# Weaving the preparations of a group's two tiles in stage 2 of a macaron layer on one core

## The chip, the cores and the metric

The kernel runs on 1 core of one Trainium2 chip. The metric is the device time of the whole program in microseconds (us), the median of several runs. TensorE (PE) multiplies matrices, with a separate row for its weight loads (PEld); VectorE (DVE), ScalarE (ACT) and GpSimd (POOL) work elementwise; SyncE (SP) issues all of this kernel's DMAs, in one queue, in program order. Each engine runs its own instructions in order, and semaphores tie them together.

## The reference, cut to what matters

The input is x of 2 batches, 2048 tokens and width 1024. A feed-forward block stands before and after an attention block:

```python
x = x + 0.5 * ffn(layernorm(x))
x = x + attn(layernorm(x))
x = x + 0.5 * ffn(layernorm(x))

def ffn(x):                                   # the token-wise part
    thought = agg of the LAST token; 4 steps of layer_norm -> d1 (1024x4096) -> gelu -> d2
    gate = sigmoid(x @ gate_w + gate_b)
    return layer_norm(x + gate * broadcast(thought @ bc_w + bc_b)) * out_gamma + out_beta

def attn(x):                                  # blocks of 128 tokens: own block and the one before
    q, k, v = split(x @ w_attn.T)
    sim = masked(q @ k2.T / 128);  a = relu(sim) ** 2
    return (a @ v2) @ w_o.T
```

## The kernel before

All tokens are cut into 32 tiles of 128 tokens, and tiles go in pairs: 16 groups of GROUP = 2 tiles, two batches in turn, from the last tokens to the first. Stage 1 (to about 713 us of the profiled execution) folds the attention's weights (wq with wk, wv with wo) and computes the first block's gates. Stage 2 (713 to 1655 us) takes the 16 groups through attention. Stage 3 (to the end) computes the second block's gates and the output. The "thought", the chain that only the last token of each batch needs, is a long series of small matmuls whose weights stream in from memory (`thought_units`); its second round is woven through stage 2 (pieces whose names begin with t_).

The order of all work is one list, PLAN, made by functions of Python. Every engine walks this list and emits its own part of each piece, so a place in the list is a place in each engine's queue. `plan_stage_2` takes for each group n the products of group n (`plan_products`, `plan_attention`) and weaves into them the preparation of group n + 1 (`plan_prep`) with `paced(..., 1.3, PE_PIECES)`: after each PE piece the next 1.3 pieces of the preparation follow. A piece ("rest",) emits nothing; it only takes a place. The last gates of stage 1 carry the preparation of group 0 in the same way.

A group from n = 3 on has 30 PE pieces: 8 q (24 matmuls 128x256 each), 9 v (three values of the four, each in thirds of 8 matmuls 128x512), 6 score, 3 v, 4 collect. Their results go to four PSUM banks in turn (`product_banks`). Banks are emptied by ACT (high part, 16 bit) and then DVE (low part): q_low is L1747, v_low L1788, score L1762, L1765 and L1777, collect L1797. In each group q takes banks 0 to 3, the three values 0 to 2, the first score 3, the second score 0, the last value 1. The score also waits for all four q_low.

A tile u of a preparation passes through:

- prep_fetch (L1020, L1024): SP fetches x (px) and the stage-1 gate (pg) of both tiles of the next group; this stands at the end of a group. The pg slot is free when the group before has been transposed.
- prep_norm (ACT L1430), prep_h (DVE L1701, needs pg), prep_beta (DVE L1708), prep_y (DVE L1714, then moments L1547 and following).
- prep_x1 (DVE L1723, L1728), prep_stats (DVE L1547 and following, then POOL), x1_store (SP L1043).
- prep_h1 (ACT L1438, L1441, needs POOL's statistics), prep_low (DVE L1738).
- group_turn (SP L1037): a transposing DMA into `gate_arena` (the first two groups: `thought_units`). The first q of a group waits for both tiles' transposes.

The thought's pieces in this stretch: t_low (DVE L1953; then SP stores the result, L993, and fetches on, L899), t_pair and t_unit (PE L1315), t_mean and t_var (PE L1285, and short DVE work).

Of the kernel before, what the change touches and what calls it, by code (L numbers as in the profile page):

```python
# [21 lines left out]
GROUP = 2  # L22
# [382 lines left out]

def plan_prep(n):

    out = []
    for i in range(GROUP):
        u = n * GROUP + i  # L410
        out += [("prep_norm", u), ("prep_h", u), ("rest",), ("prep_beta", u), ("prep_y", u), ("rest",), ("prep_x1", u),
                ("prep_stats", u), ("rest",), ("x1_store", u), ("prep_h1", u), ("rest",), ("prep_low", u),
                ("group_turn", u)]
    return out


def plan_value(n, i, h):
# [70 lines left out]
def plan_stage_2(first, last):  # L488
    out = []
    for n in range(first, last):  # L490
        out += [("prep_fetch", n + 1)]
        products, values = plan_products(n)
        out += paced(products + plan_attention(n, values), plan_prep(n + 1), 1.3, PE_PIECES)
    return out
# [61 lines left out]
def whole_plan():  # L556
# [37 lines left out]
    before = [(kind, u) for kind in ("prep_norm", "prep_beta") for u in range(GROUP)]  # L594
    prep = [("rest",)] + [("prep_norm", 1), ("prep_beta", 1)] + [("rest",)] * 3
    prep += [p for p in plan_prep(0) if p not in before]
    late = []
    for n in range(LATE):
# [1488 lines left out]
```

## Time and profile before

| | us |
|---|---|
| median of 3 runs | 1989.63 (1988.72 to 1992.05) |
| the profiled execution, its own time | 1999.55 |
| its span | 1998.3 |
| PE busy in the span | 1944.7 (97%) |
| DVE busy | 1300.3 (65%) |
| ACT busy | 662.8 (33%) |
| POOL busy | 166.4 (8%) |

The time of a run and the span of its profile differ by 1.25 us of work around the program. The profiled execution is 9.9 us longer than the median, so differences are worked out in the profiled execution and then taken off the median. A row of a timeline gives the start, the time from the first instruction's start to the last one's end, the line, the operation, the tiles and, in brackets, idle time of that engine just before and who ended it. L numbers are lines of the kernel before; in the changed kernel everything below `plan_prep` stands one line higher.

### The profile page before, as it was taken

Reading aid. Unit: us, or ns where it says so; the run is one execution under the profiler, and the core shown is the slowest. Engines: PE = TensorE matmul, PEld = TensorE weight load, DVE = VectorE, ACT = ScalarE, POOL = GpSimd, SP = SyncE. Lnnn points to the kernel's source line nnn. Section 1 sums busy time; section 2 is a strip of 40 time slices with the busy share of each in tenths; the row PEclk is TensorE's granted clock in tenths of the full one; section 3 lists DMA queues with packets and bytes.
Section 4 is the critical chain, followed back from the end, with each engine's and each line's share of the span. In section 5 each row is a group of like instructions: output and inputs, shape, how many; then the busy total and the mean of one; then the engine's idle time right before and its main releaser. Section 6 shows DMA issues by size and latency. Waiting matters only on the chain.

```text
span 1998.3 us, 30999 instructions
## 1 busy us (share of the span) xinstructions
PE 1944.7 (97%) x12136; PEld 1034.7 (52%) x12136; DVE 1300.3 (65%) x2318; ACT 662.8 (33%) x961; POOL 166.4 (8%) x278
## 2 busy tenths in 40 slices
PE   8999999999999999999999999999999999999997
PEld 3334444444444466666556566556655564444443
DVE  2656687224444666777877756757657638888887
ACT  1455456213333322224343221222112213444442
POOL 0000001000000100110100000100000001111111
PEclk9999999999999999999999999999999999999999
DMA  9899987889899753389979899998999965555552
GB/s 362 315 343 351 384 307 292 309 313 359 349 407 392 295 190 106 97 286 342 304 260 341 272 373 315 322 312 306 319 333 300 337 227 171 149 155 151 158 148 74
DMA packets 275217, 555.81 MB, mean 278 GB/s; under 512 B 149040, under 2 KB 149248, under 8 KB 274688
## 3 DMA queue, kind: packets, MB, share of 16 engines
q1 hardware_dynamic: 275072, 553.83, 79.4%
q8 instruction: 97, 1.59, 0.3%
q14 instruction: 48, 0.39, 0.1%
HBM read 406.93 MB, written 113.26 MB: 260 GB/s over the span
## 4 chain that ended last, share of the span: by engine, by line
PE 36%; DMA 7%; DVE 6%; SPq 2%; ACT 1%; issue 1%; POOL 0%; DVEq 0%; ACTq 0%
PE product_banks L1116 32%; DMA thought_units<-parts_scratch 3%; PE thought_acc L1315 2%; PE product_banks L1250 2%; DMA arena<-gate_scratch 1%; DVE bn_parts L1547 1%; DMA thought_units<-in_d_w 1%; DMA arena<-in_x 1%; DVE thought_units L1953 1%; SPq L1037 1%; SPq L899 1%; DMA gate_arena<-arena 1%; DVE arena L1728 1%; DVE arena L1723 1%; DVE arena L1714 0%
## 5 line engine op out<-in xcount | busy, mean ns | idle before, releaser
L1116 PE MATMUL product_banks<-gate_arena,arena 128*128 128x512 f16 x1536 | 347.8, 381 | 0.0
L1116 PE MATMUL product_banks<-wide_a,thought_units 128*128 128x512 f16 x1536 | 331.7, 379 | 0.0
L1116 PE MATMUL product_banks<-gate_arena,wide_a 128*128 128x256 f16 x2688 | 303.4, 274 | 8.2 <-DMA gate_arena<-arena 8.2
L1116 PE MATMUL product_banks<-wide_b,gate_arena 128*128 128x512 f16 x1344 | 299.2, 379 | 0.0
L1116 PEld LDWEIGHTS product_banks<-gate_arena,wide_a 128*128 128x128 f16 x2688 | 261.6, 98 | 54.2 <-issue 22.3
L1116 PEld LDWEIGHTS product_banks<-gate_arena,arena 128*128 128x128 f16 x1536 | 148.4, 99 | 191.8 <-issue 31.0
L1116 PEld LDWEIGHTS product_banks<-wide_a,thought_units 128*128 128x128 f16 x1536 | 150.3, 98 | 181.2
L1116 PEld LDWEIGHTS product_banks<-wide_b,gate_arena 128*128 128x128 f16 x1344 | 129.5, 98 | 157.4 <-issue 11.3
L1547 DVE BATCH_NORM_STATS2 bn_parts<-arena 128x6 f32<-128x512 f32 x256 | 164.2, 683 | 4.6
L2017 POOL TENSOR_TENSOR token_stats<-stats,minus_half 128x1 f32<-128x1 f32 x96 | 65.2, 679 | 991.8 <-DVE stats L1555 814.0
L1572 DVE SCALAR_TENSOR_TENSOR arena<-product_banks,inverse_gate,arena 128x512 f32<-128x512 f32 x64 | 48.0, 749 | 131.5 <-PE product_banks L1116 104.0
L1147 PE MATMUL product_banks<-wide_a,wide_b 128*128 128x512 f32 x256 | 120.7, 619 | 5.8 <-DMA wide_a<-in_w_attn 5.8
L2017 POOL TENSOR_TENSOR stats<-stats,minus_half 128x1 f32<-128x1 f32 x64 | 65.7, 1027 | 671.4 <-DVE stats L1555 387.0
L1453 ACT ACTIVATE gate_arena<-product_banks 128x256 f16<-128x256 f32 x128 | 41.3, 379 | 203.7 <-PE product_banks L1116 203.7
L1315 PE MATMUL thought_acc<-thought_units,thought_parts 128*6 128x512 f16 x1356 | 96.1, 379 | 6.4 <-DMA thought_units<-parts_scratch 5.0
L1459 ACT ACTIVATE arena<-product_banks 128x512 f16<-128x512 f32 x64 | 38.1, 597 | 182.8 <-PE product_banks L1116 182.8
L1493 ACT ACTIVATE arena<-arena 128x512 f32<-128x512 f32 x64 | 40.4, 632 | 168.3 <-DVE arena L1572 168.3
L1430 ACT ACTIVATE arena<-arena,token_stats 128x1024 f32<-128x1024 f32 x32 | 39.6, 1236 | 168.1 <-DMA arena<-in_x 168.1
L1701 DVE TENSOR_TENSOR arena<-arena,thought_row 128x1024 f32<-128x1024 f32 x32 | 39.0, 1219 | 84.9 <-DMA arena<-gate_scratch 84.9
L1250 PE MATMUL product_banks<-arena,key_weights 128*128 128x512 f16 x372 | 86.0, 384 | 4.7 <-DVE key_weights L1777 3.3
L1147 PEld LDWEIGHTS product_banks<-wide_a,wide_b 128*128 128x128 f32 x256 | 47.9, 196 | 67.9 <-issue 67.9
L1116 PE MATMUL product_banks<-gate_arena 128*128 128x256 f16 x672 | 78.1, 273 | 0.0
(223 smaller groups left out, 2357.5 us busy)
## 6 DMA issues: line engine op xcount, KB each, us to landing
thought_units<-parts_scratch SPq DMA_DIRECT2D x275, 512.0 KB, 7.6
thought_units<-in_d_w SPq DMA_DIRECT2D x174, 512.0 KB, 7.0
arena<-in_x SPq DMA_DIRECT2D x64, 512.0 KB, 9.3
parts_scratch<-thought_units SPq DMA_DIRECT2D x64, 512.0 KB, 6.1
x_scratch<-arena SPq DMA_DIRECT2D x64, 512.0 KB, 8.2
thought_row<-in_d_w SPq DMA_DIRECT2D x50, 512.0 KB, 7.0
arena<-x_scratch SPq DMA_DIRECT2D x40, 512.0 KB, 7.5
gate_scratch<-arena SPq DMA_DIRECT2D x32, 512.0 KB, 8.3
```

What stands on the lines that cost most here:

```text
L1116: mm = pe.matmul(bank, left(i, k), right(j, k), start=(n == 0), stop=(n == 3 * KD - 1))
L1147: mm = pe.matmul(bank_ap(key), wide_b[:, e, d * P:(d + 1) * P], wide_a[:, e, h * BANK:(h + 1) * BANK], start=(e == 0), stop=(e == KD - 1))
L1250: mm = pe.matmul(bank_ap(key), weights_of(u, side)[:, i], value_parts(other)[:, j, h * BANK:(h + 1) * BANK], start=(side == n == 0), stop= ...
L1315: mm = pe.matmul(thought_acc[at:at + PARTS * B, :], value, unit[:, part, h * BANK:(h + 1) * BANK], start=first and part == 0, stop=last an ...
L1430: act.activation(ph_slots[u % PREP_RING], px_slots[u % PREP_RING], ACT.Identity, bias=st[:, 1:2], scale=st[:, 0:1]).then_inc(h0_made, 1)
L1453: act.activation(queries[:, query_place(n * GROUP + i), 0, e - 1:e + 1, :], made[:, i], ACT.Copy, scale=QUERY_SCALE).then_inc(q_high_made, 1)
L1459: act.activation(value_parts(n * GROUP + i)[:, 0, h * BANK:(h + 1) * BANK], bank_ap(key), ACT.Copy, scale=VALUE_SCALE).then_inc(value_high, 1)
L1493: act.activation(res, res, ACT.Sigmoid).then_inc(gated_3, 1)
L1547: dve.bn_stats(bn_parts[:, h, :], source[:, h * BANK:(h + 1) * BANK]).then_inc(own.up(), 1)
L1572: dve.scalar_tensor_tensor(out=res[:, cols], in0=bank_ap(key), scalar=inverse["gate"][:, :], in1=bias[:, cols], op0=ALU.mult, op1=ALU.add) ...
L1701: dve.tensor_tensor(gb, gb, thought_row[:, GROUP_OF[u // GROUP][0], :], ALU.mult).then_inc(gate_spread, 1)
L2017: return pool.tensor_tensor(to, st[:, 2:3], minus_half[:, 0:1], ALU.pow)
```

## The change

`plan_prep` is rewritten. Before, tile u and tile u + 1 each had a run of 14 places, one after the other, with four rests each: 28 places. Now the list is written out once for the two tiles u and w, with 24 places, four of them rests: the pieces of w start inside those of u. The pieces, their instructions and their buffers are the same; only their places in the list move. At 1.3 places a PE piece, the last one, group_turn of w, comes after 18.5 PE pieces instead of 21.5.

```diff
 def plan_prep(n):
 
-    out = []
-    for i in range(GROUP):
-        u = n * GROUP + i
-        out += [("prep_norm", u), ("prep_h", u), ("rest",), ("prep_beta", u), ("prep_y", u), ("rest",), ("prep_x1", u),
-                ("prep_stats", u), ("rest",), ("x1_store", u), ("prep_h1", u), ("rest",), ("prep_low", u),
-                ("group_turn", u)]
-    return out
+
+    u, w = n * GROUP, n * GROUP + 1
+    return [("prep_norm", u), ("prep_h", u), ("rest",), ("prep_beta", u), ("prep_y", u), ("prep_norm", w), ("prep_h", w),
+            ("prep_x1", u), ("prep_stats", u), ("prep_beta", w), ("prep_y", w), ("x1_store", u), ("prep_h1", u),
+            ("prep_x1", w), ("prep_stats", w), ("prep_low", u), ("group_turn", u), ("rest",), ("x1_store", w),
+            ("prep_h1", w), ("rest",), ("rest",), ("prep_low", w), ("group_turn", w)]
```

DVE, near the end of the preparation of tiles 10 and 11 inside group 4 (931 to 990 us). Before; L1788 is a v_low of group 4, L1953 a t_low, L1762 and L1765 the first score of group 4, L1738 the prep_low of tile 11:

```order
841 L1788 SCALAR_TENSOR_TENSOR arena<-product_banks,arena 128x512
842 L1953 SCALAR_TENSOR_TENSOR thought_units<-thought_units,unit_scale 128x1024
843 L1762 SCALAR_TENSOR_TENSOR key_weights<-product_banks,score_scale,keep_own 128x128
844 L1765 SCALAR_TENSOR_TENSOR product_banks<-key_weights 128x128
845 L1762 SCALAR_TENSOR_TENSOR key_weights<-product_banks,score_scale,keep_prev 128x128
846 L1765 SCALAR_TENSOR_TENSOR product_banks<-key_weights 128x128
847 L1953 SCALAR_TENSOR_TENSOR thought_units<-thought_units,unit_scale 128x1024
848 L1738 SCALAR_TENSOR_TENSOR arena<-arena 128x1024
```

The same place in the changed kernel (lines one lower); the first L1737 is the prep_low of tile 10, the second that of tile 11, and the three v_low of group 4 stand between them:

```order
828 L1973 TENSOR_TENSOR hidden<-part_sums,d_bias 128x16 x2
829 L1546 BN_STATS bn_parts<-arena 128x6 x2
830 L1548 BN_AGGR stats<-bn_parts 128x2
831 L1551 TENSOR_SCALAR stats<-stats 128x1
832 L1556 TENSOR_SCALAR stats<-stats 128x1
833 L1737 SCALAR_TENSOR_TENSOR arena<-arena 128x1024
834 L1787 SCALAR_TENSOR_TENSOR arena<-product_banks,arena 128x512 x3
835 L1737 SCALAR_TENSOR_TENSOR arena<-arena 128x1024
836 L1952 SCALAR_TENSOR_TENSOR thought_units<-thought_units,unit_scale 128x1024
837 L1761 SCALAR_TENSOR_TENSOR key_weights<-product_banks,score_scale,keep_own 128x128
```

The prep_low of tile 11 moved ahead of two t_low and of the first score's four instructions; the three v_low moved behind all of both tiles' other preparation.

SP, the same stretch. Before; the first L1037 transposes tile 10 and the second tile 11, L1043 stores x1 of tile 11:

```order
432 L1037 DMA_TRANSPOSE gate_arena<-arena 128x16x128
433 L1058 DMA arena<-x_scratch 128x1024 x2
434 L899 DMA thought_units<-parts_scratch 128x1024 x2
435 L993 DMA parts_scratch<-thought_units 128x1024
436 L899 DMA thought_units<-in_d_w 128x1024
437 L1043 DMA x_scratch<-arena 128x1024
438 L993 DMA parts_scratch<-thought_units 128x1024
439 L899 DMA thought_units<-in_d_w 128x1024
440 L1037 DMA_TRANSPOSE gate_arena<-arena 128x16x128
```

The same place in the changed kernel:

```order
432 L1036 DMA_TRANSPOSE gate_arena<-arena 128x16x128
433 L1042 DMA x_scratch<-arena 128x1024
434 L1057 DMA arena<-x_scratch 128x1024 x2
435 L898 DMA thought_units<-parts_scratch 128x1024 x2
436 L992 DMA parts_scratch<-thought_units 128x1024
437 L898 DMA thought_units<-in_d_w 128x1024
438 L1036 DMA_TRANSPOSE gate_arena<-arena 128x16x128
439 L992 DMA parts_scratch<-thought_units 128x1024
440 L898 DMA thought_units<-in_d_w 128x1024
```

The transpose of tile 11 moved ahead of one store of the thought and its fetch, but one such pair still stands ahead of it; the store of x1 moved to just behind the transpose of tile 10. PE's own queue is the same instruction for instruction.

## Rows read from the trace of the kernel before

**Rows 1.** The page, busy time, share of the span and instructions.

```profile
PE 1944.7 (97%) x12136; PEld 1034.7 (52%) x12136; DVE 1300.3 (65%) x2318; ACT 662.8 (33%) x961; POOL 166.4 (8%) x278
```

**Rows 2.** Who PE waited for, 700 to 1660 us: total, times, longest.

```profile
PE product_banks L1116 <- DMA gate_arena<-arena: 8.2, 5, 2.7
PE thought_acc L1315 <- DMA thought_units<-parts_scratch: 5.0, 7, 2.0
PE product_banks L1250 <- DVE key_weights L1777: 3.3, 2, 2.2
PE thought_turn L1285 <- DVE thought L1993: 2.3, 3, 1.1
PE product_banks L1250 <- DVE arena L1788: 1.2, 1, 1.2
...
PE product_banks L1116 <- DVE gate_arena L1747: 0.6, 1, 0.6
```

**Rows 3.** Timeline of PE at three of these waits, start and length first.

```profile
762.28 2.29 PE L1250 MATMUL product_banks<-arena,key_weights 128*128 128x512 f16 x5 [2.21 <-DVE key_weights L1777]
...
990.54 0.80 PE L1116 MATMUL product_banks<-gate_arena,wide_a 128*128 128x256 f16 x4 [2.24 <-DMA gate_arena<-arena]
...
1472.95 1.25 PE L1116 MATMUL product_banks<-gate_arena,wide_a 128*128 128x256 f16 x10 [2.73 <-DMA gate_arena<-arena]
```

**Rows 4.** Stretches: length, busy time of the engines (instructions), granted clock, DMA share, GB/s.

```profile
762.00:766.00 4.00, 3.72 (x10) 1.40 (x11) 1.42 (x3) 0.53 (x1) 0.00 (x0) 0.57 1.06 314
...
990.50:994.00 3.50, 3.46 (x18) 2.55 (x19) 3.41 (x7) 0.00 (x0) 0.00 (x0) 0.54 0.90 294
```

**Rows 5.** Timeline of SP, issues of tiles 10 and 11, then of tile 27.

```profile
965.53 6.06 SPq L1037 DMA_TRANSPOSE gate_arena<-arena  x1
...
979.95 0.32 SPq L993 DMA_DIRECT2D parts_scratch<-thought_units  x1
...
981.37 6.96 SPq L1037 DMA_TRANSPOSE gate_arena<-arena  x1
...
1459.15 11.55 SPq L1037 DMA_TRANSPOSE gate_arena<-arena  x1
```

**Rows 6.** Timeline of DVE inside group 4, the preparation of tiles 10 and 11.

```profile
943.87 1.23 DVE L1701 TENSOR_TENSOR arena<-arena,thought_row 128x1024 f32<-128x1024 f32 x1 [7.91 <-DMA arena<-gate_scratch]
...
964.87 1.22 DVE L1701 TENSOR_TENSOR arena<-arena,thought_row 128x1024 f32<-128x1024 f32 x1
966.01 0.68 DVE L1788 SCALAR_TENSOR_TENSOR arena<-product_banks,arena 128x512 f16<-128x512 f32 x1
...
976.28 1.28 DVE L1953 SCALAR_TENSOR_TENSOR thought_units<-thought_units,unit_scale 128x1024 f16<-128x1024 f32 x1
977.47 0.35 DVE L1762 SCALAR_TENSOR_TENSOR key_weights<-product_banks,score_scale,keep_own 128x128 f32<-128x128 f32 x1
...
979.99 1.23 DVE L1738 SCALAR_TENSOR_TENSOR arena<-arena 128x1024 f16<-128x1024 f32 x1
```

**Rows 7.** Stretches from the first L1701 to the last L1738 of a preparation; columns as in rows 4.

```profile
943.87:981.22 37.35, 37.35 (x266) 23.18 (x264) 34.80 (x56) 16.32 (x24) 4.46 (x6) 1.00 0.91 308
1424.39:1459.13 34.74, 34.22 (x255) 22.04 (x253) 31.27 (x69) 10.21 (x18) 3.23 (x7) 1.00 0.71 258
```

**Rows 8.** Timeline of PE around the scores of group 4.

```profile
970.39 1.04 PE L1116 MATMUL product_banks<-gate_arena 128*128 128x256 f16 x8
...
972.32 4.54 PE L1116 MATMUL product_banks<-gate_arena 128*128 128x256 f16 x40
```

**Rows 9.** Timeline of DVE: end of group 1's preparation, start of group 13's.

```profile
758.35 1.23 DVE L1738 SCALAR_TENSOR_TENSOR arena<-arena 128x1024 f16<-128x1024 f32 x1 [2.08 <-ACT arena L1441]
...
1424.39 1.23 DVE L1701 TENSOR_TENSOR arena<-arena,thought_row 128x1024 f32<-128x1024 f32 x1 [11.17 <-DMA arena<-gate_scratch]
```

**Rows 10.** Stretches by DMA share; columns as in rows 4.

```profile
1150.00:1250.00 100.00, 98.37 (x800) 63.22 (x799) 60.50 (x129) 20.24 (x39) 6.73 (x17) 1.00 0.99 345
...
1550.00:1600.00 50.00, 49.34 (x358) 26.64 (x356) 31.93 (x67) 10.04 (x17) 3.46 (x9) 1.00 1.01 334
```

## The prediction, written before the changed kernel ran

> **What bounds the kernel now.** I read the page's busy shares first, then who PE waited for in stage 2, then the timelines of PE, DVE and SP at the largest of those waits, and last the busy time of DVE over one preparation. PE is busy 1944.7 us of the span, 97% [rows 1]. The change moves no PE instruction, so what it can give is only PE's idle time in stage 2, and what it can take is new idle time there. The list of waits is the whole prize: 20.6 us from 700 to 1660 us if its lines are added, of which the largest is 8.2 us in five waits for a transpose into `gate_arena` [rows 2]. Each of these five is the first q of a group waiting for the second tile of its own preparation; two of them are seen at 990.54 (2.24 us) and 1472.95 (2.73 us) [rows 3]. The next lines are the thought's weights (5.0 us in seven waits), the score's low parts L1777 (3.3 us in two), the thought's DVE step L1993 (2.3 us in three), one v_low L1788 (1.2 us) and one q_low L1747 (0.6 us) [rows 2].
>
> Behind the transposes stands DVE. From the first instruction of tile 10 to the last of tile 11 it is busy 34.80 of 37.35 us, for tiles 26 and 27 31.27 of 34.74 us [rows 7]. So the second tile is late for two reasons: its pieces stand late in the list, and DVE has little air. Both count below.
>
> A second price hangs on two of the waits. Right behind the wait that ended at 762.28 the granted clock is 0.57 over 4 us, and behind the one that ended at 990.54 it is 0.54 over 3.5 us [rows 3, 4]; elsewhere in stage 2 it is at full speed. That is the lower of the two levels (1.2 instead of 2.4 GHz) for most of these stretches; the work lost is 4.0 x 0.43 = 1.7 us and 3.5 x 0.46 = 1.6 us. The wait at 1472.95 was longer and no low stretch followed, so a wait of this size may or may not bring one.
>
> **The transposes (removed: 8.2 us).** How much earlier is the second tile? Take group 4. In the changed order two t_low and the first score's four instructions no longer stand ahead of tile 11's L1738. By starts in rows 6, a t_low takes 977.47 - 976.28 = 1.2 us, twice 2.4; the four of the score end where the second t_low started, 978.65, so 1.2 us. The same busy time less these: 34.8 - 3.6 = 31.2, so L1738 of tile 11 would end at 943.87 + 31.2 = 975.1 instead of 981.2, if DVE never waits. It cannot come before the three v_low, whose last product is complete when the first score starts at 970.39 [rows 8]; that bound is the earlier one, so DVE decides. On SP one store and one fetch of the thought still stand ahead of the transpose: the store waits for a t_low that ends 1.2 us behind L1738, and store and fetch take 1.4 us (979.95 to 981.37 [rows 5]). So the transpose issues at 975.1 + 1.2 + 1.4 = 977.7 instead of 981.37, 3.7 us earlier. PE waited 2.24 us. The wait goes, with 1.4 us to spare. For tile 27 no such store stands ahead: 31.27 us of DVE less 1.3 for the first score ends L1738 at 1454.4 instead of 1459.1, 4.7 us earlier against a wait of 2.73 us [rows 3, 7]. The other three waits are shorter, 8.2 - 2.24 - 2.73 = 3.2 us together. I take all 8.2 us. From the other side the bound is 0: SP's issue of one transpose takes 6.06 to 11.55 us [rows 5], and the two of a group now stand closer, so a second one could queue behind a slow first.
>
> **The clock (removed: 3.3 us).** If the waits before 762.28 and 990.54 go, both low stretches go, 1.7 + 1.6 = 3.3 us. Bounds: 0 if some other gap brings them back, 3.3.
>
> **The collects (removed: 4.5 us).** At 758.35 DVE stood idle 2.08 us for ACT's half of tile 3's preparation, with L1738 ahead of the score's low part in its queue [rows 9]; PE then waited 2.21 us [rows 3]. In the new order this L1738 stands a PE piece behind the start of the first score, its ACT part two pieces before that, so it neither waits nor stands in the way: 2.2 us. The second L1777 wait (3.3 - 2.2 = 1.1 us) and the v_low one (1.2 us) come at the end of groups whose L1738 ran up to the collects; they go for the same reason, 2.3 us. Bounds 0 and 4.5.
>
> **What stays.** The waits for the thought's weights (5.0 us), for L1993 (2.3 us) and the one for q_low (0.6 us) are not touched by design. The three rests fewer in each tile and the second tile's store of x1, moved to just behind the first transpose on SP, cost nothing by themselves: a rest emits nothing, and the first tile's transpose, now three PE pieces later, was issued at 965.53 for a q at 990.54 [rows 3, 5]: 25 us, of which three of a group's 30 pieces (some 6 us) are a quarter.
>
> **What is added (about 5 us).** DVE now does both tiles' work before the first v_low of a group. In group 4 what stands behind this v_low inside the old stretch is two more v_low (0.6 us each by start to start [rows 6]), L1738 of tile 11 (1.2), two t_low (2.4) and the first score (1.2): 6.0 us. So it ends at 943.87 + 34.8 - 6.0 = 972.7 instead of 966.7. The second score needs its bank. It starts after the 16 remaining matmuls of the first, 16 x 4.54/40 = 1.8 us behind 972.32, at 974.1 [rows 8]: a margin of 1.4 us, where there were 7.4. In the four groups with t_low on DVE I allow 0.75 us each, 3 us in all; in the later ones the two t_low pairs ahead of it are absent and the margin is some 4 us wider. The thought's short DVE steps (L1993 and others) meet a denser DVE in the first half of a group and a freer one in the second; I allow 1 us. The DMAs are busy 0.99 and 1.01 of two stretches of stage 2 [rows 10], and all transfers must now fit a shorter time: 1 us more for the thought's weights. Bounds of the whole term: -2 (the fetches of the next group stand behind the last transpose on SP, so they go out earlier and DVE's stall at L1701, 7.91 us and 11.17 us [rows 6, 9], shrinks) and 15.
>
> **The sum.** 8.2 + 3.3 + 4.5 = 16.0 us removed, 5 us added, net 11 us: the profiled execution would take 1988.5 us instead of 1999.55, and the median 1989.63 - 11.0 = 1978.6 us. Its own range runs from 16 + 2 = 18 us less (1972) to 5 us less (1985).
>
> **Rivals.** *The gain is given back to the DMAs.* If the stretch from 850 to 1600 us is held by the thought's transfers, only what lies before 850 us is gained, 2.2 + 1.7 = 3.9 us: 1985.7 us. For it: the shares of 0.99 and 1.01 [rows 10]. Against: PE waits for these weights only 5.0 us in all [rows 2], and the share from 943.87 to 981.22 is 0.91 [rows 7]. A page of the Trainium skill speaks for it: "DMA: Bandwidth & Descriptors", section "Issuing engines are not separate DMA queues", says that all DMAs run on the same 16 engines and interleave there. The trace agrees in so far as the same transpose takes SP 6.06 us in one group and 11.55 us in another.
>
> *The second tile is not earlier.* If the store and fetch ahead of it on SP and the slow first transpose eat the 3.7 to 4.7 us, the 8.2 us and the 1.6 us of clock stay: 16.0 - 9.8 - 5 = 1.2 us less, 1988.4 us. Against: the margins above are worked out with them.
>
> *Slower: the first v_low comes too late.* DVE runs in order, and in all 13 groups from n = 2 on the second tile's L1701, which waits for its own fetch, now stands ahead of q_low and v_low of the running group. If DVE is L us later than I reckon at the first v_low, the second score waits L - 1.4 us in each: with L = 3, 13 x 1.6 = 20.8 us, less 16 gained, 4.8 us more: 1994.4 us. It is even at L = 2.6. For it: DVE busy 34.80 of 37.35 us [rows 7] and stalls of 7.91 and 11.17 us at L1701 [rows 6, 9]. Against: both fetches of a group are issued together, so the second is there soon after the first, and the groups without t_low have a wider margin. The Trainium skill, "TensorE: Matmul & The Clock Gate", section "Architectural detail: the array is 16x 32x32, not 1x 128x128", states that ScalarE and VectorE queues are strict FIFO; this is the mechanism of that rival, and the trace agrees: the q_low of group 4 ran only after the 7.91 us stall.
>
> **How the numbers follow.** The forecast has 0.70, the DMAs 0.13, the second tile not earlier 0.09, slower 0.08. This kernel's measurement can tell about 0.2% from no change, 4 us; faster means below 1985.65. The forecast and a little of the DMA rival lie there: 0.71. Same: the rest of it and the second tile, 0.21. Slower: 0.08. The range leaves out the slower rival and the far ends: 1971.5 to 1989.
>
> **What would show it.** In the profile after, the waits of PE for `gate_arena<-arena` should be under 1 us in all, the granted clock should not fall around the starts of groups 1 and 5, PE's idle time from 713 to 1655 us should be near 13 us instead of 20.6, and the transposes of second tiles should land 3 to 5 us ahead of the first q. New waits of PE on L1787 (v_low) at the second score would show the added term; above 15 us in all they would make the prediction wrong. So would waits for the thought's weights above 10 us.

## The result, and the profile after

The changed kernel is slower. Its median is 2026.17 us (2021.73 to 2028.32, four runs) against 1990.84 us (1988.72 to 1997.18, four runs) of the kernel before: ratio 1.0157, 95% interval 1.0138 to 1.0175. The ratio, which this text goes by, is some 31 us; the two medians stand 35.3 us apart. The forecast was 1978.6 us, the range ended at 1989.0.

The page of the changed kernel, the busy line (as [rows 1]) and the DMA's mean rate:

```profile
PE 1954.4 (96%) x12136; PEld 1038.1 (51%) x12136; DVE 1300.4 (64%) x2318; ACT 662.9 (33%) x961; POOL 193.1 (10%) x278
...
DMA packets 275217, 555.81 MB, mean 274 GB/s; under 512 B 149040, under 2 KB 149248, under 8 KB 274688
```

PE is busy 9.7 us longer with the same 12136 matmuls. DVE and ACT have not changed. The bytes are the same, and their rate fell only because the run is longer. The next two fences give all of stage 2 as one stretch, of after and then of before (columns as in [rows 4]).

```profile
700.00:1683.00 983.00, 942.72 (x6974) 592.13 (x6973) 644.33 (x1282) 243.94 (x399) 99.83 (x159) 0.98 0.81 273
```

```profile
700.00:1655.00 955.00, 933.55 (x6982) 589.64 (x6981) 646.67 (x1283) 244.00 (x400) 74.35 (x158) 1.00 0.84 281
```

The stretch grew by 28 us, as much as the whole span (2026.6 instead of 1998.3). So the loss is in stage 2, and it has two parts: PE stands idle 40.3 instead of 21.4 us (+18.9), and it works 9.2 us longer because its granted clock was lower. It stood on its low level for 37.5 us of this stretch, in seven pieces; before it was 6.8 us in two.

Who PE waited for after the change, 650 to 1700 us (total, times, longest; as [rows 2], lines one lower):

```profile
PE thought_acc L1314 <- DMA thought_units<-parts_scratch: 23.8, 10, 5.5
PE thought_turn L1284 <- DVE thought L1992: 4.7, 1, 4.7
PE product_banks L1115 <- DVE arena L1787: 4.5, 2, 2.6
PE product_banks L1249 <- DVE key_weights L1776: 1.4, 1, 1.4
PE product_banks L1115 <- DVE gate_arena L1746: 1.4, 1, 1.4
PE product_banks L1249 <- DVE arena L1787: 1.3, 1, 1.3
PE thought_acc L1304 <- DMA thought_units<-in_agg_w: 0.9, 1, 0.9
PE thought_turn L1284 <- DVE squares L1875: 0.8, 1, 0.8
PE product_banks L1115 <- DMA gate_arena<-arena: 0.8, 1, 0.8
```

The waits for the transposes, which the change was expected to remove, fell from 8.2 to 0.8 us. In their place stand 23.8 us for the thought's weights (5.0 before) and one wait of 4.7 us in the thought's DVE chain. By the starts of the groups' first q, groups 3 to 8 take 379.9 us instead of 357.5, and groups 9 to 15 with the end of the stage 430.0 instead of 424.8.

Two of the three largest new waits lie at the ends of groups 3 and 4 (the third, 4.67 us in the thought's DVE chain, comes further below). Timeline of PE after the change:

```profile
930.94 1.88 PE L1314 MATMUL thought_acc<-thought_units,thought_parts 128*6 128x512 f16 x16 [5.53 <-DMA thought_units<-parts_scratch]
...
994.25 1.88 PE L1314 MATMUL thought_acc<-thought_units,thought_parts 128*6 128x512 f16 x16 [3.87 <-DMA thought_units<-parts_scratch]
```

and timeline of SP ahead of the second of them, where [rows 5] has the same place of before:

```profile
975.53 0.43 SPq L992 DMA_DIRECT2D parts_scratch<-thought_units  x1
976.01 0.49 SPq L898 DMA_DIRECT2D thought_units<-in_d_w  x1
981.78 1.58 SPq L1036 DMA_TRANSPOSE gate_arena<-arena  x1
983.40 1.29 SPq L1042 DMA_DIRECT2D x_scratch<-arena  x1
984.80 1.83 SPq L1057 DMA_DIRECT2D arena<-x_scratch  x2
986.73 0.86 SPq L898 DMA_DIRECT2D thought_units<-parts_scratch  x2
```

From 976.50 to 981.78 SP issues nothing: it stands at the transpose of tile 10. What it waits for is on DVE, in the timeline of that engine:

```profile
952.71 1.22 DVE L1700 TENSOR_TENSOR arena<-arena,thought_row 128x1024 f32<-128x1024 f32 x1 [6.26 <-DMA arena<-gate_scratch]
...
980.54 1.22 DVE L1737 SCALAR_TENSOR_TENSOR arena<-arena 128x1024 f16<-128x1024 f32 x1
981.67 1.28 DVE L1787 SCALAR_TENSOR_TENSOR arena<-product_banks,arena 128x512 f16<-128x512 f32 x2
985.30 0.69 DVE L1787 SCALAR_TENSOR_TENSOR arena<-product_banks,arena 128x512 f16<-128x512 f32 x1 [2.35 <-ACT arena L1458]
985.90 1.22 DVE L1737 SCALAR_TENSOR_TENSOR arena<-arena 128x1024 f16<-128x1024 f32 x1
```

L1737 of tile 10 comes 27.8 us after the first L1700, since DVE has most of tile 11's preparation ahead of it by then. In the kernel before it came 17 us after it (960.81, with the first L1701 at 943.87). The transpose waits for it, and behind the transpose, in SP's queue, stands the fetch of the thought's weights that PE is going to need. The fetch goes out at 986.73, PE wants the weights at 990.38 and gets them at 994.25. Before, the same pair of fetches went out at 972.78. Group 4 itself begins 6.2 us later now (937.51, before 931.31), so counted from its first q the pair goes out after 49.2 us instead of 41.5:

```profile
971.70 0.99 SPq L1058 DMA_DIRECT2D arena<-x_scratch  x2
972.78 0.86 SPq L899 DMA_DIRECT2D thought_units<-parts_scratch  x2
```

The wait at the end of group 3 is read in the same way, and there the groups start almost together (873.73 and 873.15): the first transpose goes out at 914.13 instead of 903.33, the pair of fetches behind it at 922.74 instead of 914.29; the second of the pair lands at 930.80, and PE goes on at 930.94.

Over the stage SP stood for prep_low this long (waits of SP's queue, 700 to 1660 us), after the change and then before:

```profile
SPq L1036 <- DVE arena L1737: 121.4, 19, 16.6
```

```profile
SPq L1037 <- DVE arena L1738: 81.2, 19, 10.1
```

Counted as the gaps in SP's issues just before each transpose, it is 109 us after the change, 96 ahead of first tiles and 13 ahead of second ones, and 85 before, 46 and 39.

Each of the seven waits of 2.2 us or more in this stage ends in, or is followed by, a stretch at a low clock; none of the shorter ones has such a stretch to itself. At the two above, after the change (columns as in [rows 4]; the first stretch lies for the most part inside the wait itself, so PE is busy little in it):

```profile
928.00:932.00 4.00, 1.06 (x12) 0.42 (x16) 0.00 (x0) 0.00 (x0) 0.00 (x0) 0.50 1.12 277
930.90:935.50 4.60, 4.56 (x25) 1.54 (x26) 0.38 (x1) 0.00 (x0) 0.00 (x0) 0.60 1.14 286
994.20:998.50 4.30, 4.25 (x22) 1.30 (x23) 0.00 (x0) 1.15 (x1) 0.00 (x0) 0.50 1.13 358
```

The thought's 16 matmuls take 1.88 us there and 1.04 us at full clock elsewhere. Such stretches, 30.7 us more of them than before, are where PE's 9.7 us come from.

### The profile page after: what moved, and what is told of

Read it like the earlier page. It is cut to its first block, busy times and chain, and to the rows that moved or that the text cites. A ratio compares the mean times of both kernels' runs of the same rounds, so it can differ in the third digit from the quotient of the medians.

```text
span 2026.6 us, 30999 instructions
## 1 busy us (share of the span) xinstructions
PE 1954.4 (96%) x12136; PEld 1038.1 (51%) x12136; DVE 1300.4 (64%) x2318; ACT 662.9 (33%) x961; POOL 193.1 (10%) x278
## 2 busy tenths in 40 slices
DMA packets 275217, 555.81 MB, mean 274 GB/s; under 512 B 149040, under 2 KB 149248, under 8 KB 274688
## 4 chain that ended last, share of the span: by engine, by line
PE 37%; DVE 6%; DMA 5%; SPq 3%; issue 1%; ACT 1%; POOL 0%; ACTq 0%; DVEq 0%
PE product_banks L1115 33%; PE thought_acc L1314 2%; PE product_banks L1249 2%; DMA thought_units<-parts_scratch 2%; SPq L1036 2%; DMA arena<-gate_scratch 2%; DMA thought_units<-in_d_w 1%; DVE bn_parts L1546 1%; DVE thought_units L1952 1%; SPq L898 1%; DMA arena<-in_x 1%; DVE arena L1727 1%; DVE arena L1722 0%; DVE arena L1707 0%; DVE arena L1713 0%
## 5 line engine op out<-in xcount | busy, mean ns | idle before, releaser
L1115 PEld LDWEIGHTS product_banks<-wide_b,gate_arena 128*128 128x128 f16 x1344 | 130.3, 99 | 160.0 <-issue 15.7
L2016 POOL TENSOR_TENSOR token_stats<-stats,minus_half 128x1 f32<-128x1 f32 x96 | 81.7, 851 | 1127.3 <-DVE stats L1554 916.1
L1314 PE MATMUL thought_acc<-thought_units,thought_parts 128*6 128x512 f16 x1356 | 99.0, 389 | 25.1 <-DMA thought_units<-parts_scratch 23.8
L1787 DVE SCALAR_TENSOR_TENSOR arena<-product_banks,arena 128x512 f16<-128x512 f32 x64 | 43.3, 687 | 91.3 <-ACT arena L1458 91.3
L1700 DVE TENSOR_TENSOR arena<-arena,thought_row 128x1024 f32<-128x1024 f32 x32 | 39.0, 1218 | 85.1 <-DMA arena<-gate_scratch 85.1
```

The costliest lines, as they stand in the source:

```text
L1115: mm = pe.matmul(bank, left(i, k), right(j, k), start=(n == 0), stop=(n == 3 * KD - 1))
L1314: mm = pe.matmul(thought_acc[at:at + PARTS * B, :], value, unit[:, part, h * BANK:(h + 1) * BANK], start=first and part == 0, stop=last an ...
L1787: dve.scalar_tensor_tensor(out=parts[:, 1], in0=bank_ap(key), scalar=VALUE_SCALE, in1=parts[:, 0], op0=ALU.mult, op1=ALU.subtract).then_in ...
L2016: return pool.tensor_tensor(to, st[:, 2:3], minus_half[:, 0:1], ALU.pow)
```

## The experiments

Two theories stood against each other. **SP's queue**: the first tile's transpose waits longer for its prep_low, and the thought's fetches stand behind it. **DVE**: with four rests fewer and both tiles' work first, DVE is too dense or late for what PE and the thought need from it. In the expectations A and S are the first; B is the second; C says that SP's order is harmless and that only DVE's late prep_low costs, by making SP stand; D says that it is the second transpose, early on SP in front of a fetch that PE needs; E is a loss that stays in its group, F one that drags on, G one that is the same in every group. "Idle" below is PE's idle time from 700 us to the start of stage 3, "low" the time at the low clock there; before has 21.4 and 6.8 us, after 40.3 and 37.5. Ratios are against the kernel before on the same chip, with the 95% interval. u is a group's first tile, w its second.

**Fewer rests, old order.** Still tile after tile, two rests of four taken out of each.

```diff
-        out += [("prep_norm", u), ("prep_h", u), ("rest",), ("prep_beta", u), ("prep_y", u), ("rest",), ("prep_x1", u),
-                ("prep_stats", u), ("rest",), ("x1_store", u), ("prep_h1", u), ("rest",), ("prep_low", u),
+        out += [("prep_norm", u), ("prep_h", u), ("rest",), ("prep_beta", u), ("prep_y", u), ("prep_x1", u),
+                ("prep_stats", u), ("x1_store", u), ("prep_h1", u), ("rest",), ("prep_low", u),
```

> The old order, tile after tile, but with four rests instead of eight (24 places), so the second tile's transpose stands 12 PE pieces ahead of the next group as in the changed kernel, and the first tile's 21 ahead (20 before, 17 in the changed kernel). Theory A (what costs 35 us is the first tile's transpose, which is late and stands on SP in front of fetches that PE needs 11 us later): no cost here, and the 8.2 us of waits for transposes go: 1975 to 1990 us. Theory B (it is the shorter, denser preparation on DVE, whatever the order of the tiles): slower than before, 2005 us or more.

Measured: 2017.0 against 1995.46 us, 1.0109 (1.0084 to 1.0134); idle 32.9, low 27.3. The denser list alone, without weaving, costs 21.5 us (B's side). Its waits are of another kind: 7.9 us for L1993, 6.9 for v_low, 7.6 for the thought's weights, and none at the end of group 3. So the plan before is finely set, and moving the preparation in it in either manner has a price.

**Woven, but the first tile as early as before.** 24 places as in the change, with prep_low and group_turn of u back at their old distance from the end, those of w as in the change.

```diff
...
+            ("prep_x1", u), ("prep_stats", u), ("prep_h", w), ("x1_store", u), ("prep_h1", u), ("prep_beta", w),
+            ("prep_low", u), ("group_turn", u), ("prep_y", w), ("rest",), ("prep_x1", w), ("prep_stats", w),
+            ("x1_store", w), ("prep_h1", w), ("rest",), ("rest",), ("prep_low", w), ("group_turn", w)]
```

> Woven, 24 places, but the first tile's prep_low and transpose stand where they stood before (21 and 20 PE pieces ahead), the second tile's where the changed kernel has them (13 and 12). Theory A: PE's waits for the thought's parts fall from 23.8 us to under 8 and the time to 1980 to 1995 us. Theory B (dense DVE through weaving): stays above 2010 us, with waits on DVE or for the parts above 15 us.

Measured: 2003.69 against 1995.46 us, 1.0043 (1.0023 to 1.0063); idle 30.4, low 17.1. Of 31 us, 22 are gone, with the same number of rests, and the waits for the thought's weights fell from 23.8 to 10.3 us; both numbers lie between what A and B had forecast. The wait at the end of group 3 is gone. In group 4 SP now issues the transpose of u at 971.42 and the thought's fetches at 979.35:

```profile
971.42 5.88 SPq L1035 DMA_TRANSPOSE gate_arena<-arena  x1
977.35 0.58 SPq L1041 DMA_DIRECT2D x_scratch<-arena  x1
978.04 1.22 SPq L1056 DMA_DIRECT2D arena<-x_scratch  x2
979.35 1.58 SPq L897 DMA_DIRECT2D thought_units<-parts_scratch  x2
```

PE still waits 3.08 us for these weights, at 987.89. The run is the strongest evidence that the late first tile costs most of it. But this edit moves the tile on DVE and on SP together, and puts pieces of w behind it that stood ahead of it in the change.

**SP's order alone.** Five kernels let SP walk a list of its own, made with another plan_prep, while all other engines keep theirs:

```diff
+SP_PLAN = whole_plan()
...
-        for kind, *a in PLAN:
+        for kind, *a in SP_PLAN:
             if kind == "start":
```

The kernel before, SP in the changed order:

> All engines as in the kernel before, SP alone walks the order of the changed kernel. Theory A in its narrow form (the places on SP alone do it; the first transpose is ready but issued late, in front of the fetches): the waits for the thought's parts rise to 12 us or more, 2005 to 2020 us. Theory C (the order of SP is harmless, what costs is that DVE makes the first tile's prep_low 10 us later, so that SP stands at its transpose): within 8 us of before, 1983 to 1999 us.

Measured: 2012.86 us, 1.0090 (1.0074 to 1.0106); idle 29.8, low 27.3; 14.8 us for the thought's weights. No instruction of DVE, ACT or PE moved, and 17.4 us are lost, as A had it. In group 4 the thought's fetches go out at 977.19, 49.7 us after the group's first q (927.47), as late as in the changed kernel, and PE waits 6.86 us for them. But this isn't a share of the change's 31 us: there is no wait at the end of group 3, and SP stands 29 us ahead of first transposes and 54 us ahead of second ones, the other way round than in the changed kernel (96 and 13), since here the second one is asked for before DVE has made its tile.

The changed kernel, SP in the old order:

> All engines as in the changed kernel, SP alone walks the order of the kernel before: the first tile's transpose stands three PE pieces earlier on SP than DVE's prep_low for it. Theory A in its narrow form: back to 1985 to 2000 us. Theory C: SP now stands at the first transpose from an even earlier place until DVE has made prep_low, with still more fetches behind it: 2026 us or more.

Measured: 2036.05 us, 1.0208 (1.0187 to 1.0230); idle 46.2, low 37.5. SP stands 148 us ahead of first transposes, which are now asked for at the old early place while DVE makes them late, as C had it (whose range the kernel above had missed, 1983 to 1999 us). The order must fit the time at which tiles are ready, on both queues.

The woven list with the early first tile, SP in the old order:

> The engines as in e2 (woven, 24 places, first tile's prep_low where it was before, second tile's three PE pieces earlier), SP alone in the order of the kernel before: the second transpose stands 9 pieces ahead of the next group, behind the thought's fetch that the collects need, and finds its tile ready. Theory D (each place of a transpose on SP ahead of that fetch costs, because the next fetches stand behind its issue of 6 to 12 us): the cost of e2 goes, 1980 to 1996 us. Theory B (the denser DVE costs by itself): 2000 us or more, with waits on DVE as in e2 and few for the parts.

Measured: 2004.79 against 1993.57 us, 1.0057 (1.0039 to 1.0075); idle 26.5, low 10.2. The same as with SP in its own woven order (1.0043) within the intervals, where D had forecast that the cost would go. The waits for weights are down to 4.3 us; those for transposes are back, 10.0 us.

The kernel before, only the transpose of w four places earlier on SP (ahead of w's own store of x1 and of the thought's stores that stood before it), and, apart from it, only that of u four places later on SP, both from group 1 on:

> The kernel before; on SP alone the second tile's transpose moves from 9 to 12 PE pieces ahead of the next group (its prep_low is at 10 on DVE), past the thought's fetch. Theory D: the waits for the parts rise to 12 us or more and most of the 17 us of e3 is here, 2005 to 2015 us. Theory A (it is the first tile's transpose): within 5 us of before.

> The kernel before; on SP alone the first tile's transpose moves from 20 to 17 PE pieces ahead of the next group, with its tile ready since long. Theory A: 2003 us or more and waits for the parts above 12 us. Theory D: little, since no fetch that PE needs soon is passed: within 5 us of before.

Measured: w earlier 2007.47 us, 1.0065 (1.0046 to 1.0084), idle 28.8, low 17.1; u later 1998.49 us, 1.0023 (1.0010 to 1.0036), idle 22.9, low 13.7. By medians 13.9 and 4.9 us, about the 17.4 us of both together, as D had it. So of SP's order alone it is the second transpose that costs most. The first is plain to read. The transpose of w is asked for before w is ready, and SP stands (waits of SP's queue in that kernel, where before had 81.2 us; L1052 is its transpose):

```profile
SPq L1052 <- DVE arena L1753: 139.6, 24, 13.8
```

PE's list of waits in the same kernel:

```profile
PE thought_acc L1330 <- DMA thought_units<-parts_scratch: 12.1, 11, 2.4
PE thought_turn L1300 <- DVE thought L2008: 6.3, 3, 4.6
PE thought_turn L1338 <- DVE t_wide L1975: 3.3, 1, 3.3
```

No wait for a transpose is left, and it is slower by 14 us: 8.2 us of waits for transposes were exchanged for more waits for the thought.

**The changed kernel, the first transpose held behind the next fetch of the thought on SP.** From group 3 on.

```diff
+        if piece[0] == "group_turn" and piece[1] % GROUP == 0 and piece[1] >= 3 * GROUP:
+            held.append(piece)
+            continue
...
-        for kind, *a in PLAN:
+        for kind, *a in SP_PLAN:
```

> The changed kernel; on SP alone the first tile's transpose is held back, from group 3 on, behind the next fetches of the thought's products (at the latest to just before the second's). If the fetches behind the first transpose are what costs in the changed kernel (theory A), PE's waits for the parts fall from 23.8 us to under 12 and the time from about 2030 to 2005 us or less. If the cost is the late DVE or the second transpose, the time stays above 2018 us.

Measured: 2024.02 us, 1.0153 (1.0123 to 1.0183); idle 38.0, low 27.3. A cure by SP's queue alone failed (A had forecast 2005 us or less). It did what it should in the place at which it was aimed: SP stands 62.9 instead of 121.4 us for prep_low, and the wait at the end of group 3 is 1.22 instead of 5.53 us.

```profile
921.00 1.04 PE L1332 MATMUL thought_acc<-thought_units,thought_parts 128*6 128x512 f16 x16 [1.22 <-DMA thought_units<-parts_scratch]
```

```profile
912.87 10.02 SPq L1054 DMA_TRANSPOSE gate_arena<-arena  x2
922.94 0.81 SPq L1010 DMA_DIRECT2D parts_scratch<-thought_units  x1
```

But the two transposes then stand back to back and hold the queue for 10.02 us, and what comes behind them is late instead. The wait at the end of group 4 is gone. Waits for the weights went from 23.8 to 15.7 us, while waits for v_low rose from 5.8 to 8.3 us and those of L1340 for t_wide from 0.3 to 3.8 us. The time stayed.

**Where in the stage.** The woven list in some groups only, the old one in the others.

```diff
+def plan_prep(n):
+
+    return plan_prep_woven(n) if 3 <= n <= 8 else plan_prep_old(n)
```

Groups 0 to 2:

> The changed order for the preparations of groups 0 to 2 alone, the old one for all others. In the changed kernel's profile group 3 begins only 0.5 us later than in the kernel before. Theory E (the loss is local, it adds up over the groups): 0 to 4 us slower than before. Theory F (a late start of one group drags through all that follow): 15 us or more.

Groups 3 to 8:

> The changed order for the preparations of groups 3 to 8 alone, where the thought's weights are still split on DVE (t_low) and DVE is busiest. In the changed kernel's profile the stretch from group 3 to group 9 takes 22.6 us more than before. Theory E: 18 to 30 us slower than before, the greater part of the 31 to 35 us. Theory G (weaving costs the same in every group): 12 to 15 us, 6 of 16 groups.

Groups 9 to 15:

> The changed order for the preparations of groups 9 to 15 alone. DVE has no t_low there and is busy about 65% instead of 80%. The changed kernel's profile has 5.2 us more from group 9 on. Theory E: 2 to 9 us slower. Theory G: 14 us or more.

Measured: 1.0013 (1.0001 to 1.0025), 1.0118 (1.0098 to 1.0138) and 1.0024 (1.0013 to 1.0034), at some 1995 us that is 2.6, 23.5 and 4.8 us. The shares add up to 1.0155, where the whole change has 1.0157: the loss is local, as E had it, and nothing is built up from group to group. The middle kernel shows the two waits of groups 3 and 4 again:

```profile
927.49 1.88 PE L1330 MATMUL thought_acc<-thought_units,thought_parts 128*6 128x512 f16 x16 [6.47 <-DMA thought_units<-parts_scratch]
...
991.01 1.54 PE L1330 MATMUL thought_acc<-thought_units,thought_parts 128*6 128x512 f16 x16 [3.52 <-DMA thought_units<-parts_scratch]
```

Three quarters of the loss lie with these six preparations, which run inside groups 2 to 7. Inside groups 3 to 6 t_low runs on DVE beside them, and SP has stores of its results and more fetches in its queue. In groups 9 to 15, where the forecast saw a wide margin, the change still gains nothing.

**The better version only where it should do no harm.** Early first tile, woven, in groups 9 to 15.

> The order of e2 (woven, the first tile's prep_low kept early) for the preparations of groups 9 to 15 alone, the old one elsewhere. The waits of PE from group 9 on sum to 5.0 us in e2's profile and 7.6 us in the kernel before, so the best hope is 2 to 3 us faster than before, 0.1%; if a denser DVE costs even here, 3 us or more slower.

Measured: 1994.67 us (12 runs) against 1994.48 (29 runs), 1.0002 (0.9989 to 1.0014). No difference. None of the kernels beats the one before.

**The thought's fetches on another engine's queue.** ACT issues the 224 fetches of split weights of this round, at the same places of the list; SP keeps all else. If only SP's queue makes the change slow, it should then cost nothing.

```diff
+                for n in a[0].fetch:
+                    if on_act(a[0], n):
+                        fetch_unit(n, act)
```

In the old order:

> The kernel before, but in the second thought's round the fetches of split weights (thought_units<-parts_scratch) are issued by ACT at the same places of the list, no longer by SP; nothing else moves. It is the base for e14 and e15. SP no longer holds such a fetch behind a transpose, ACT pays 0.4 to 1 us for each issue (some 16 a group). PE's waits for the parts fall from 5.0 us to about 2; the time is 1980 to 2005 us.

In the changed one:

> The changed kernel with these fetches issued by ACT. Theory S (SP's queue: fetches behind a transpose that waits for DVE): PE's waits for the parts fall from 23.8 us to under 8, and the time comes within 12 us of e13. Theory B (DVE's denser work by itself): it stays 20 us or more above e13, with waits on DVE lines.

In the woven one with the early first tile:

> The order of e2 (woven, first tile's prep_low early) with these fetches issued by ACT. Theory S: the 8.6 us of e2 go and the second tile's earlier transpose pays, at or below e13. Theory B: 8 us or more above e13.

Measured: 2101.17 us (1.0539, 1.0488 to 1.0591), 2055.38 us (1.0287, 1.0245 to 1.0328) and 2066.41 us (1.0366, 1.0311 to 1.0420); idle 113.5, 74.2 and 86.1. All three are far slower, which no theory had expected. The waits for the weights are 18.0, 16.3 and 38.0 us, where S had under 8 for the second; those for the transposes 77.1, 41.8 and 32.7. In the first one PE waits for the transposes above all:

```profile
PE product_banks L1122 <- DMA gate_arena<-arena: 77.1, 9, 16.1
PE thought_acc L1321 <- DMA thought_units<-parts_scratch: 18.0, 7, 4.8
```

One of these waits, on PE, and the issue of the transpose that it waits for, on SP:

```profile
1011.63 4.64 PE L1122 MATMUL product_banks<-gate_arena,wide_a 128*128 128x256 f16 x21 [11.55 <-DMA gate_arena<-arena]
```

```profile
992.39 6.29 SPq L1042 DMA_TRANSPOSE gate_arena<-arena  x1
```

The transpose is issued at 992.39 and PE goes on at 1011.63, 19 us later. Over the 28 transposes into `gate_arena` the mean from issue to landing is 12.6 us with a longest of 29.9, against 8.7 and 14.2 in the kernel before. ACT also stood 140 us at these fetches, with its own work on the tiles behind them. So the edit brought new effects in, larger than the one that it was to measure, and it doesn't decide between the theories. It tells one thing: as soon as transposes are the late thing, the order of the change is worth much (2055 instead of 2101 us, 46 us). The idea behind the change was sound for a kernel in which transposes are scarce; here only 8.2 us of PE's time, and the low clock behind one of the waits, hung on them.

## Why the prediction was wrong, point by point

**What bounds the kernel**: right. PE's queue is unchanged, and all of the difference is PE's idle time in stage 2 and its clock.

**The transposes**: right in the result (8.2 to 0.8 us), not in the working, and in the main by luck. In group 4 tile 11's L1737 was to end 31.2 us after the first L1700; it ended at 987.12, 34.4 us after it. 2.35 us of that DVE waited for ACT's half of the third value, so the bound by the v_low, which the prediction set aside with "so DVE decides", did count. The second transpose went out 36.5 us after the first L1700 (989.24 less 952.71), where 33.8 were forecast and 37.5 were measured before; counted from the group's first q it is even later (51.7 us, before 50.1). Over groups 3 to 14 it goes out 48.7 us after the first q in the mean, before 49.5, and lands after 59.0 instead of 59.3 us. PE no longer waits for it because these groups themselves have grown, from 60.5 to 62.8 us in the mean, by the new waits.

**The clock**: its sign was wrong. 3.3 us were to come back; instead the low stretches grew from 6.8 to 37.5 us, since new waits took the place of the old ones. The bound of this term was zero below, with the words "0 if some other gap brings them back". It had to allow for a loss, as new waits bring new low stretches.

**The collects**: the wait for L1777 at 762 us went, those for L1776 and v_low are 1.4 and 1.3 us at other places. But two new waits for L1787 (4.5 us in all, one of 2.57 us at 735.82) are about as large. Together that is 7.2 us where 4.5 had stood: no gain of 4.5 us but a loss of 2.7.

**What stays**: this is the step that failed. "The first tile's transpose, now three PE pieces later" was held to cost nothing, because the q that reads it comes 25 us later. This asked who needs the tile, and not who stands behind its transpose on SP: a store of x1, a fetch of x1 and the fetches of the thought. Nor were three PE pieces the whole delay. DVE had tile 11's work to do first, and L1737 of tile 10 moved by 11 us against the first L1700 of the group (27.8 instead of 16.9 us). SP stood 96 instead of 46 us ahead of first transposes. The waits for the thought's weights, named in the same step as "not touched by design", are where the time went: 5.0 to 23.8 us. (The text also said three rests fewer in each tile; it is two in each, eight to four.)

**What is added**: the v_low of group 4 ends 982.3 - 952.7 = 29.6 us after the first L1700, where 28.8 were forecast; that estimate held. The waits for v_low are 5.8 us in all (those of the paragraph above, not to be counted twice), 4.6 more than before, where 3 were allowed. For the thought's DVE steps and its fetches 1 us each were allowed. They cost 2.4 us (L1992, 2.3 to 4.7) and 18.8 us. The three make 25.8 us, above the upper bound of 15 us for the whole term, for which the prediction gave no working. The lower bound of -2 us, from fetches that go out earlier, came out the other way: in group 4 DVE's first L1700 began 15.2 us after the group's first q (952.7 less 937.5), where it had been 12.6 us (943.87 less 931.31). DVE's stalls at this line, which were to shrink, are 85.1 us in the changed kernel and 84.9 before.

**The rivals.** The slower one (0.08) had the right side and the wrong mechanism: PE doesn't wait for v_low in group after group. The DMAs' rival was near to the place of the new waits, but its reason, the transfers' capacity, isn't what the trace shows: 555.81 MB at 274 instead of 278 GB/s, DMA share 0.81 against 0.84. A fetch of the thought's weights lands 7.2 us after its issue in both (median, 850 to 1600 us). The weights come late because they are asked for late. In one place capacity may have its part: the gate's fetch at 1126.09 (below) took 12.9 us to land, before 8.7. The mark that the prediction itself set, waits for the thought's weights above 10 us, was met. The Trainium skill ("TensorE: Matmul & The Clock Gate", section "Architectural detail: the array is 16x 32x32, not 1x 128x128") says that ACT's and DVE's queues are strictly first in, first out. The prediction worked this out for DVE alone. SP's issues, of which that section says nothing, stand in the order of the program too: at 976.50 SP stops at the transpose, and nothing behind it goes out before 981.78. There it decided.

**What is shown and what stays open.** Shown: where the first tile comes early again, 22 of 31 us are gone; SP's order alone, with no other engine's changed, costs 17.4 us, though mainly by its second transposes, which are asked for too early there and not in the changed kernel; the loss is local and three quarters of it lie in groups 3 to 8. In groups 3 and 4 the chain from DVE's L1737 over SP's standing transpose to the late fetch and PE's wait is read step by step. The wait at the end of group 3 is there with the whole change (5.53 us) and with groups 3 to 8 alone (6.47), is 1.22 us where SP holds the transpose back, and is absent where the first tile is early or SP's order alone is changed. A second chain comes from the second transpose: behind it, as it holds SP from 1113.02 to 1120.95, six fetches of the thought go out ahead of the gate's at 1126.09 (two before, since four went ahead of the transpose), DVE stands 10.05 us at L1700 for it (6.11 before), and the thought's step L1992 behind it lets PE wait 4.67 us at 1136.56. The same wait is 3.82 us with SP alone in the changed order and 4.62 us with w's transpose alone earlier on SP; where SP keeps the second transpose in its old place, none for this line is over 1.1 us. So it needs no change on DVE. Timeline of DVE in the changed kernel:

```profile
1139.03 1.22 DVE L1700 TENSOR_TENSOR arena<-arena,thought_row 128x1024 f32<-128x1024 f32 x1 [10.05 <-DMA arena<-gate_scratch]
...
1141.00 0.17 DVE L1992 TENSOR_TENSOR thought<-thought,squares 128x16 f32<-128x16 f32 x1
```

Open is how much of the 23.5 us in groups 3 to 8 belongs to SP's order and how much to DVE's own lateness. The two aren't independent: SP's old order makes the changed kernel worse (1.0208), a later transpose on SP leaves it as it was (1.0153) though both of the waits at which it was aimed are gone or short, and the fetches on ACT's queue brought their own effects. Open as well is why fewer rests alone, in the old order, cost 21.5 us; its waits lie in the thought's chain and at v_low, but no run takes them apart.

## What to carry to other kernels

In an engine that issues transfers in order, a transfer costs what stands behind it while it waits for its data. Before moving a transfer or its producer, write down for each wait on that queue when its data is ready and which transfer behind it is needed first, for the first tile of a pair just as for the last. And where a plan is balanced to a few microseconds, the short waits that a shift brings count more than their length: here 18.9 us of new idle time came with another 9.7 us of slower work.

## What the runs showed of the hardware

A second queue wasn't free for the transposes. With 117 of the 556 MB issued by ACT instead of SP, the transposing DMAs into `gate_arena` landed after 12.6 us in the mean (longest 29.9) instead of 8.7 (14.2), and the kernel was 5.4% slower. The same fetches, now on ACT's queue, landed after 10.0 instead of 7.7 us in the mean, and those of x on SP's after 12.1 instead of 8.6. In the changed order with and without ACT's queue it is 10.8 and 8.0 us for the transposes, 8.0 and 7.8 for the weights, 7.4 and 8.7 for x. How much of the 5.4% is this, and how much is ACT's standing at its fetches, no run takes apart. From the page of that kernel, section 3 (queue: packets, MB, share):

```profile
q1 hardware_dynamic: 242816, 436.37, 62.9%
q10 hardware_dynamic: 32256, 117.45, 16.5%
```

The Trainium skill ("DMA: Bandwidth & Descriptors", section "Issuing engines are not separate DMA queues") has all issuing engines share the same 16 DMA engines. That fits a lack of any gain; that the transposes lost most, in both orders, is what these runs add. Why they did isn't shown.

A transposing DMA also holds its issuer. In the kernel before SP's issue of one into `gate_arena` took from 1.3 to 11.9 us, with a median of 6.6; the issue of a plain transfer in this stage had a median of 0.4 us.

And a low stretch of the clock doesn't follow from a wait's length alone: in the kernel before, waits of 2.21 and 2.24 us were followed by one and one of 2.73 us was not [rows 3, 4], nor was one of 3.18 us at 930.21 with the change in groups 9 to 15 alone. In the changed kernel a wait of 5.53 us had the clock down before PE went on (0.50 from 928 to 932 us).
